# A new work order within a state-space tile, one product moved to GpSimd, and two additions moved to TensorE

## The reference, cut to what matters

```python
def mamba_block(seq, ...):
    u, z = split(einsum('bld,ed->ble', seq, in_proj_w))
    u = silu(sum(up[:, k:k + L, :] * conv_w[:, k] for k in range(4)) + conv_b)
    dt, Bm, Cm = split(einsum('bld,ed->ble', u, x_proj_w), [DT_RANK, DT_RANK + 16])
    dt = softplus(einsum('blr,dr->bld', dt, dt_proj_w) + dt_proj_b)
    A = -exp(A_log)
    def step(h, (dt_t, B_t, C_t, u_t)):
        h = exp(dt_t[:, :, None] * A) * h + (dt_t * u_t)[:, :, None] * B_t[:, None, :]
        return h, einsum('bdn,bn->bd', h, C_t)
    y = scan(step) + u * D
    return einsum('bld,ed->ble', y * silu(z), out_proj_w)
x = x + mamba_block(x);  x = x + experts(x)      # twice
```

## Time and profile before

| | us |
|---|---|
| median of 3 runs | 1975.07 (1973.82 to 1977.28) |
| the profiled execution | 1973.6 |
| its span, first to last instruction | 1971.8 |
| VectorE busy in the span | 1359.6 (69%) |
| TensorE matmuls busy | 1445.4 (73%) |
| GpSimd busy | 1138.6 (58%) |
| ScalarE busy | 928.1 (47%) |

### The profile page before, as it was taken

One profiled execution on the slowest core, in us unless ns is written; L12 is line 12 of the kernel. 1 busy time (PEld: TensorE's weight loads), 2 busy tenths in 40 slices (PEclk: granted clock), 3 DMA queues, 4 the chain that ended last, 5 costly groups with the idle time before them and its releaser, 6 DMA issues. The chain is left out here.

```text
span 1971.8 us, 28551 instructions
## 1 busy us (share of the span) xinstructions
PE 1445.4 (73%) x7776; PEld 980.9 (50%) x7777; DVE 1359.6 (69%) x1913; ACT 928.1 (47%) x1695; POOL 1138.6 (58%) x788
## 2 busy tenths in 40 slices
PE   6666766667656599999956766666667662799993
PEld 4333333333314499999834333333333222799992
DVE  2899999999995422222143999999999967444443
ACT  6666677667743011111136666677666731011111
POOL 0687788888880244444302888888878850355540
PEclk9889898998968699999968788998998866899996
DMA  3655566555638110111034565566555634111114
GB/s 110 147 135 121 129 144 146 125 126 134 145 79 354 54 41 32 38 37 36 26 126 98 129 138 121 129 143 139 134 121 135 148 136 188 38 48 48 47 41 152
DMA packets 75964, 217.61 MB, mean 110 GB/s; under 512 B 11856, under 2 KB 27408, under 8 KB 72592
## 3 DMA queue, kind: packets, MB, share of 16 engines
q1 hardware_dynamic: 67664, 194.53, 38.9%
q0 software_dynamic: 8256, 22.56, 3.5%
HBM read 178.34 MB, written 38.70 MB: 110 GB/s over the span
## 5 line engine op out<-in xcount | busy, mean ns | idle before, releaser
L669 POOL TENSOR_TENSOR L_hc<-L_h,L_cbq 128x1536 f32<-128x1536 f32 x192 | 660.1, 3438 | 210.6 <-DVE L_h L587 207.5
L492 ACT ACTIVATE ps<-L_dwq,L_negA 128x384 f32<-128x384 f32 x768 | 426.7, 574 | 227.4 <-DVE L_h L587 215.5
L364 PE MATMUL ps<-L_hc,same 128*32 128x384 f32 x1536 | 190.0, 571 | 238.9 <-POOL L_hc L669 238.9
L574 DVE TENSOR_TENSOR L_dbu<-L_dwq,ps 128x768 f32<-128x768 f32 x288 | 270.7, 941 | 29.4 <-DVE L_carry L649 13.1
L587 DVE TENSOR_TENSOR_SCAN L_h<-ps,L_h,L_dbu 128x384 f32<-128x384 f32 x288 | 275.0, 1002 | 12.9 <-ACT ps L492 12.8
L587 DVE TENSOR_TENSOR_SCAN L_h<-ps,L_carry,L_dbu 128x384 f32<-128x384 f32 x288 | 274.2, 1001 | 6.5 <-DVE L_dbu L574 4.7
L364 PEld LDWEIGHTS ps<-L_hc,same 128*32 128x32 f32 x1536 | 31.5, 113 | 358.2 <-POOL L_hc L669 324.3
L1151 DVE COPY Xn<-L_w 128x2048 f32 x86 | 107.6, 1253 | 117.1 <-PE ps L1101 108.3
L1134 ACT ACTIVATE L0e_hT<-ps 128x512 f32<-128x512 f32 x86 | 51.3, 597 | 267.2 <-PE ps L1101 267.2
L678 POOL TENSOR_TENSOR L_dbp<-L_dwq,L_cbq 128x768 f32<-128x768 f32 x96 | 175.1, 1824 | 0.0
L323 PE MATMUL ps<-Xn,L_fold 128*128 (+1 forms) x480 | 103.3, 368 | 89.2 <-DVE L_dw L595 89.2
(11 more groups left out here) (278 smaller groups left out, 2301.4 us busy)
## 6 DMA issues: line engine op xcount, KB each, us to landing
L_dwq<-dw_rows SPq DMA_DIRECT2D x192, 384.0 KB, 6.2
L_cbq<-cb_rows SPq DMA_DIRECT2D x192, 240.0 KB, 9.9
dw_rows<-L_dw SPq DMA_DIRECT2D x48, 384.0 KB, 2.3
L_w<-in_up SPq DMA_DIRECT2D x16, 1024.0 KB, 11.7
L_w<-in_down SPq DMA_DIRECT2D x8, 1024.0 KB, 26.6
tok_rows<-Xn SPq DMA_DIRECT2D x6, 768.0 KB, 13.1
L0s_got<-results SPq DMA_DIRECT2D x18, 256.0 KB, 2.9
L1s_got<-results SPq DMA_DIRECT2D x18, 256.0 KB, 3.5
```

Source lines behind the costliest of these rows:

```text
L364: mm = nc.tensor.matmul(y_ps[g * QW:(g + 1) * QW, :], same[:, 0:QW], hc[:, (k % 2) * Q + g, :], start=False, stop=(k == Q - 1))
L492: nc.scalar.activation(da(r, c), dwq[:, r, c % Q, 0, :], ACT.Exp, scale=negA[:, 0, c:c + 1]).then_inc(sem["da"], 1)
L574: nc.vector.tensor_tensor(dbu[:, at:at + 2, :], dwq[:, r, 2 * i:2 * i + 2, 1, :], spread(b_ps(r, k)), ALU.mult).then_inc(sem["dbu"], 1)
L669: nc.gpsimd.tensor_tensor(hc[:, at:at + Q, :], h[:, Q * k:Q * k + Q, :], cbq[:, r, k, :].unsqueeze(1).to_broadcast([P, Q, T]), ALU.mult).t ...
```

## The change

- GpSimd makes one more pair of dt*u*B products (scans 10 and 11): three `times_b` a tile, the first at the tile's head, ahead of `times_c(t, 0)`. VectorE makes five pairs. The row of B that this needs is a sixth row of `cbq` (QR = 6, 288 KB a load where it was 240), and `dbu` and `dbp` get a buffer for every scan in place of a ring.
- `lost` goes: TensorE adds e with the identity and g with a negated identity (`minus`), four matmuls of 384 columns where there were three. They now stand at the end of tile t for t+2, which is the same place of TensorE's queue as before, behind `sum_y(t, 2)`.
- `residual` goes: `project_out` starts with a matmul of the identity and X (192 columns), and ScalarE copies the sum back to X (`take_x`, after decay 14).
- `carry` stays for the start alone. States have a column more, and a scan begins from the last column of the tile before, or from the added one at an image's start.
- Order: on VectorE `times_u(t+1)` moves from behind scan 3 to behind scan 0, `gate(t-1)` from behind scan 5 to behind scan 3. On ScalarE the silus move from behind decay 7 to behind decay 6. On TensorE the head of a tile is written anew.

```diff
-QR = Q + 1
+QR = Q + 2
+SILU_AT = 6
             def add_log(t):
                 pe.wait_ge(sem["l"], t + 1)
                 nc.tensor.matmul(ua_ps, ident[:], sp["l"][:], start=False, stop=False)
-                pe.wait_ge(sem["lost"], t + 1)
-                nc.tensor.matmul(ua_ps, ident[:], sp["a"][:], start=False, stop=True).then_inc(sem["dt"], 1)
+                pe.wait_ge(sem["g"], t + 1)
+                nc.tensor.matmul(ua_ps, ident[:], sp["e"][:], start=False, stop=False)
+                nc.tensor.matmul(ua_ps, minus[:], sp["g"][:], start=False, stop=True).then_inc(sem["dt"], 1)
             def project_out(t):
                 pe.wait_ge(sem["yz"], t + 1)
+                x = X[:, :, bass.ds(t * PT, PT)].rearrange("p i (h w) -> p h i w", w=SIDE)
+                nc.tensor.matmul(zb_ps[:, 0:T // 2].rearrange("p (h i w) -> p h i w", i=2, w=SIDE), ident[:], x,
+                                 start=True, stop=False)
...
+            def take_x(t):
+                act.wait_ge(sem["out"], t + 1)
+                x = X[:, :, bass.ds(t * PT, PT)].rearrange("p i (h w) -> p h i w", w=SIDE)
+                nc.scalar.copy(x, zb_ps[:, 0:T // 2].rearrange("p (h i w) -> p h i w", i=2, w=SIDE)).then_inc(sem["res"], 1)
...
             def tile(t, r, p, slot, last):        # VectorE
                 for j in range(N // 2):
                     k, i = (j + 1) // 2, (j + 1) % 2
-                    if k < Q - 1:
+                    if 2 * k + i < 5:
                         times_b(t, r, p, k, i)
                     elif j == N // 2 - 1 and not last:
                         times_b(t + 1, 1 - r, p + r, 0, 0)
                     scan(t, 2 * j, slot)
+                    if j == 0 and not last:
+                        times_u(t + 1, 1 - r, [(s_dw_row[r], 16 * (p + 1))])
                     scan(t, 2 * j + 1, slot)
-                    if j == 1 and not last:
-                        times_u(t + 1, 1 - r, [(s_dw_row[r], 16 * (p + 1))])
                     if not (isinstance(t, int) and t == 0):
-                        if j == 2:
+                        if j == 1:
                             gate(t - 1, 1 - r)
-                        if j == 6:
-                            residual(t - 1)
...
-                    nc.vector.tensor_copy(carry[:, 1, :], h[:, :, T - 1]).then_inc(sem["carry"], 1)
-                    dve.wait_ge(sem["carry"], p + 2)
...
             def tile(t, r, p, last):              # GpSimd
+                times_b(t, r, p, 0)
                 for k in range(Q):
                     times_c(t, r, p, k)
                     if k < 2:
-                        times_b(t, r, p, k)
-                    if k == 2 and not last:
-                        lost(t + 2)
+                        times_b(t, r, p, k + 1)
```

More of the change, by code:

```diff
@@ L258, in mamba @@
         sem = {k: new(f"{L}_{k}") for k in
-               ("u_in z_in u zs bc dt_in bc_out abs relu e f g l lost dt dt_out w b dbu dbu_p da scan carry hc skip y yz out "
+               ("u_in z_in u zs bc dt_in bc_out abs relu e f g l dt dt_out w b dbu dbu_p da scan carry hc skip y yz out "
                 "res").split()}
@@ L269, in mamba @@
         diagD = sb("diagD", [P, P])
+        minus = sb("minus", [P, P])
         negA = sb("negA", [P, 2, N])
         w_dt = sb("w_dt", [P, P])
-        carry = sb("carry", [P, 2, N])
+        carry = sb("carry", [P, N])
         tok = sb("tok", [P, 16])
@@ L281, in mamba @@
         dwq = sb("dwq", [P, 2, Q, 2, T])
-        dbu = sb("dbu", [P, 6, T])
-        dbp = sb("dbp", [P, Q, T])
-        h = sb("h", [P, N, T])
+        dbu = sb("dbu", [P, 10, T])
+        dbp = sb("dbp", [P, 6, T])
+        h = sb("h", [P, N, T + 1])
         hc = sb("hc", [P, 2 * Q, T])
@@ L398, in _ @@
             spread_b(0, 0, 1)
+            add_relu(1)
+            add_log(1)
             pe.wait_ge(s_tok, 7)
@@ L403, in tile @@
                 first = isinstance(t, int) and t == 0
+                spread_b(t, r, 2)
+                if more == 2:
+                    u_in(t + 2, img2, (0, 1))
+                if not first:
+                    sum_y(t - 1, 1 - r, Q - 1)
+                if more == 2:
+                    u_in(t + 2, img2, (2, 3, 4))
                 if more:
-                    add_relu(t + 1)
-                    add_log(t + 1)
                     pe.wait_ge(sem["bc_out"], t + 2)
@@ L409, in tile @@
                     z_in(t + 1, img1)
[L410 to L414, removed]
                 skip(t, r)
-                sum_y(t, r, 0)
-                if more:
-                    spread_b(t + 1, 1 - r, 0)
                 if more == 2:
@@ L422, in tile @@
                     project_bc(t + 2, r)
+                sum_y(t, r, 0)
+                if more:
+                    spread_b(t + 1, 1 - r, 0)
                 sum_y(t, r, 1)
@@ L434, in tile @@
                 sum_y(t, r, 2)
+                if more == 2:
+                    add_relu(t + 2)
+                    add_log(t + 2)
             def pair(p):
@@ L534, in tile @@
                         take_dt(t + 1, [(s_dw_row[r], 16 * (p + 1))])
-                    if c == 7 and more:
+                    if c == SILU_AT and more:
                         nc.scalar.preload_act_table_set(SILU)
@@ L540, in tile @@
                         nc.scalar.preload_act_table_set(EXP_LN)
+                    if c == 14 and not (isinstance(t, int) and t == 0):
+                        take_x(t - 1)
                     if more != 2:
@@ L559, in _ @@
             tile_pairs(act, pair)
+            take_x(NT - 1)
         @block.vector
@@ L567, in times_b @@
                     dve.wait_ge(s_dw[r], 64 * (p + 1))
[L568 to L573, removed]
+                at = 4 * k + 2 * i
+                wait(dve, sem["scan"], (t - 1) * N + at + 2)
                 nc.vector.tensor_tensor(dbu[:, at:at + 2, :], dwq[:, r, 2 * i:2 * i + 2, 1, :], spread(b_ps(r, k)),
@@ L577, in scan @@
             def scan(t, c, slot):
-                k, g = c // Q, c % Q
+                k = c // Q
                 dve.wait_ge(sem["da"], t * N + c + 1)
-                if k < Q - 1:
-                    dve.wait_ge(sem["dbu"], 6 * t + c // 2 + 1)
+                if c < 10:
+                    dve.wait_ge(sem["dbu"], 5 * t + c // 2 + 1)
                 else:
-                    dve.wait_ge(sem["dbu_p"], 2 * t + g // 2 + 1)
+                    dve.wait_ge(sem["dbu_p"], 3 * t + (c - 10) // 2 + 1)
                 wait(dve, sem["hc"], Q * (t - 1) + k + 1)
[L585 to L588, removed]
+                first = h[:, c, T - 1:T] if slot is None else h[:, c, T - slot:T - slot + 1] if isinstance(slot, int) \
+                    else h[:, c, bass.ds(T - slot, 1)]
+                nc.vector.tensor_tensor_scan(h[:, c, 0:T], da(t % 2 if isinstance(t, int) else int(slot is None), c),
+                                             dbu[:, c, :] if c < 10 else dbp[:, c - 10, :], first, ALU.mult, ALU.add
                                              ).then_inc(sem["scan"], 1)
@@ L602, in gate @@
                 nc.vector.tensor_tensor(yz[:], zs[:, r, :], y_ps, ALU.mult).then_inc(sem["yz"], 1)
[L604 to L608, removed]
             nc.vector.tensor_tensor(fold[:].rearrange("p g d -> p (g d)"), par("in_u"), par("taps"), ALU.mult
@@ L612, in _ @@
             nc.vector.tensor_scalar(diagD[:], ident[:], par("D"), None, ALU.mult).then_inc(s_fold, 1)
+            nc.vector.tensor_scalar(minus[:], ident[:], -1.0, None, ALU.mult).then_inc(s_fold, 1)
             times_u(0, 0, ())
             dve.wait_ge(s_tok, 6)
-            nc.vector.tensor_tensor(carry[:, 1, :].rearrange("p (k g) -> p k g", k=Q),
+            nc.vector.tensor_tensor(carry[:].rearrange("p (k g) -> p k g", k=Q),
                                     m["ones"][:, 0:N].rearrange("p (k g) -> p k g", k=Q),
@@ L618, in _ @@
             dve.wait_ge(sem["carry"], 1)
-            nc.vector.tensor_tensor(carry[:, 0, :].rearrange("p (k g) -> p k g", k=Q),
-                                    carry[:, 1, :].rearrange("p (k g) -> p k g", k=Q),
+            nc.vector.tensor_tensor(h[:, :, T].rearrange("p (k g) -> p k g", k=Q),
+                                    carry[:].rearrange("p (k g) -> p k g", k=Q),
                                     ps[:, 5, Q:2 * Q].unsqueeze(1).to_broadcast([P, Q, Q]), ALU.mult).then_inc(s_tok, 1)
@@ L676, in times_b @@
                     pool.wait_ge(s_dw[r], 64 * (p + 1))
[L677 to L682, removed]
+                wait(pool, sem["scan"], (t - 1) * N + 12 + 2 * i)
+                groups, row = (2, Q + 1) if i == 0 else (2 * i - 2, Q)
+                nc.gpsimd.tensor_tensor(dbp[:, 2 * i:2 * i + 2, :], dwq[:, r, groups:groups + 2, 1, :],
+                                        spread(cbq[:, r, row, :]), ALU.mult).then_inc(sem["dbu_p"], 1)
             q = {k: tok[:, 2 + i:3 + i] for i, k in enumerate("arefgl")}
@@ L1370, in pack @@
     state = g("x_proj_w")[4:].reshape(2, Q, Q, P)
```

(2 more changed lines are left out.)

17 lines of the change are left out of this document (5 added, 12 removed).

## The result

The changed kernel takes 2025.82 us (median of 4 runs, 2023.23 to 2030.42) against 1976.14 us before (4 runs): a ratio of 1.0255, 95% interval 1.0234 to 1.0277, so 2.6% slower. The forecast was 2028 us. The profiled execution spans 2021.4 us, 49.6 us more than before.

A forecast was written before the change was run, and what follows sets the result against it. VectorE's queue bounds the kernel at 22.28 us a tile; after the change a closed chain does, at 23.6. (23.6 - 22.28) x 22 - 2.0 is +27.0 us a layer, +54 on 1973.6: 2028 us, range 2002 to 2063.

The forecast's parts named there:

- a closed chain: Loop from one times_u to the next through VectorE, GpSimd, TensorE and take_dt: 18.92 us before, 23.22 us after.
- The wait: VectorE waiting before times_u for ScalarE's take_dt: 2.5 to 4 us a tile, nearly 44 tiles, 110 to 170 us.
- VectorE's step, 10.04 us: VectorE's queue from start of times_u to end of scan 7: 6.44 us before, 3.60 us added.
- GpSimd's step, 8.61 and 0.08 us: From scan 7's end: 0.08 us to GpSimd's start, then 8.61 us to the end of group 2's C product, unchanged.
- TensorE's step at full clock, 3.16 + 0.70 us: From GpSimd's end to take_dt's start: sum and three softplus additions 3.16 us, plus 0.70 for the extra matmul.
- The slow clock, 0.4 us a tile: TensorE's half-clock spells on the additions before take_dt: 0.4 us a tile added, between bounds of 0 and 1.2.
- 23.6 us a tile: Forecast tile period in the state-space blocks: the 23.22 us chain with the slow-clock allowance, against 22.28 before.
- The small parts at no cost: GpSimd's third B product, take_x and silu waits, identity matmul on X, and larger cbq load: all taken as 0.
- Faster rival: GpSimd runs quicker while VectorE stands still; 0.94 us shorter chain breaks even, 2.5 us less gives 1900 us; chance 0.05.
- Slow clock at each turn: Rival: TensorE's slow clock locks onto the softplus additions every tile, chain 25.3 us, kernel 2103 us; chance 0.12.

The follow-up runs named there:

- cutting the chain at one place: Changed kernel with TensorE's softplus additions for tile t+2 put ahead of sum_y(t, 2): 1896.49 us, ratio 0.9616 to the kernel before.
- the move alone: Kernel before with only times_u moved, from behind scan 3 to behind scan 0: 2063.13 us, ratio 1.0457.

## Why the prediction was right, step by step

- *VectorE bounds the kernel, and the next bound is a closed chain.* Right: four steps add up to a tile's length, and cutting the chain at one place gave 129 us. The wait was where it was foretold: without the starts of the two layers 136.2 us in 44 tiles, 3.1 us a tile, against "nearly 44 tiles, 110 to 170 us" and 2.5 to 4 us in each.
- *VectorE's step, 10.04 us*: measured 10.15.
- *GpSimd's step, 8.61 and 0.08 us*: measured 8.17. Too high by 0.5 us, because the longer row of the states made each of its two C products 0.27 us quicker. The prediction read the new column as a place for the start value and gave it no price.
- *TensorE's step at full clock, 3.16 + 0.70 us*: 3.72 at best, 3.80 in many tiles. The fourth addition costs 0.64.
- *The slow clock, 0.4 us a tile*: measured 4.46 - 3.72 = 0.74. Too low; the kernel before has 4.18 - 3.08 = 1.10 by the same measure. The reasoning was that `u_in` would hardly wait any more; it waits half as long as before, 44.8 us for 89.2, but the two waits for GpSimd stayed, and the spells met the additions in 24 of 44 tiles, about as often as before (25). This term was 0.34 us too low and VectorE's 0.11, while GpSimd's was 0.52 too high and the full-clock step 0.14, so that 23.6 us a tile for 23.48 is in part luck.
- *The small parts at no cost*: right on the whole. ScalarE waited 14.3 us in 11 times for `project_out` between 60 and 600 us, and VectorE's waits for decays are 16.5 us in 21 times (14.6 in 31 before). The load of `cbq` lands after 10.7 us, not 12. It is not free at the start of a layer, where GpSimd's first B product now stands ahead of everything else and waits 16.0 and 17.3 us for it; no wait of VectorE falls on that product. There VectorE's waits for `dwq` grew from 4.6 to 14.8 us, but its waits for TensorE just ahead of them shrank from 19.1 to 10.6, so from the first `times_u` to the first scan the two layers lost 0.2 and 1.5 us. One wait was not foreseen: TensorE stands in front of `project_dt` for ScalarE's silu, 70.9 us in 46 times (1.4 in 2 before). It lies outside the chain: in the tile from 315.30 us on TensorE waits again, 3.04 us for GpSimd, before the next y sum.
- *Faster rival (GpSimd quicker while VectorE stands still)*: GpSimd was quicker, but because of its row length, and by 0.5 us of the 0.94 that would break even.
- *Slow clock at each turn*: not in the changed kernel; with the move alone TensorE's step was slow in 44 of 44 tiles.

## What to carry to other kernels

When the busiest engine gets less work, ask which loop from tile to tile is next, and add its steps up from start to start in the timeline; its length is a floor under the period that no saving on the busy engine moves, unless the saving lies inside the loop. Moving an instruction earlier in a queue shortens nothing if what it needs is not earlier too: what stood in front of it, here 3.6 us of work, then waits behind it. Before moving the consumer up, move the producer up: additions whose inputs were ready stood behind a sum that waited for another engine, and putting them ahead of it was worth 6%.

## What the runs showed of the hardware that was not expected

- The GpSimd product of 4 rows of 384 columns takes 3.17 us when the states' rows are 385 columns apart and 3.44 us when they are 384, 392 or 416 apart (192 instructions in each kernel). So the slow product needs neither packed rows (416) nor a distance that is a multiple of 32 columns (392). Whether every odd distance is quick, and why, stays open: one odd distance was run. The two-input B products, whose rows kept their places, took 1.82 us throughout.
- How often TensorE's slow spells meet the same place of a loop depends on the loop: they met the additions in 24 of 44 tiles in the changed kernel, in 44 of 44 in the kernel where `times_u` alone had moved, and in 2 of 44 with eight short unused matmuls in two of the changed kernel's stops, where the granted clock over layer 0 rose from 0.89 to 0.94.
